# A graph layer in one TensorE queue: the warm-up on zeros becomes 3 wide and 75 narrow products

## What is computed

```
xn = layernorm(x)
q, k, v = (xn @ w.T + b  for w in wq, wk, wv)
q2, k2, v2 = (… @ wi.T + bi for wiq, wik, wiv)            # 16 heads of 64
mask = -inf [384, 384]; mask[src, dst] = softplus(weight of the edge's type)   # 12,288 edges
gnn = softmax(q2 k2.T / 8 + mask) v2 @ wo.T + bo
mix = (sum(phi(xn Wq + bq) * phi(xn Wk + bk)) per head) * (xn Wv + bv) @ Wo + bo
x = x + gnn + mix
x = x + base(layernorm(x)) + conv[e](up[e](relu(down[e](layernorm(x)))))
```

## Time and profile before

| | us |
|---|---|
| median of 3 runs | 499.51 |
| lowest, highest | 494.93, 501.0 |
| the profiled execution, its own time | 493.77 |
| its span, first to last instruction | 491.8 |
| TensorE busy | 468.4 (95%) |
| DVE, ACT, POOL busy | 338.6, 256.0, 160.4 |
| mean granted TensorE clock | 0.976 |

### The profile page before, as it was taken

The page is one execution under the profiler, slowest core; times in us unless marked ns, Lnnn a source line. Parts: engine busy times, 40 slices in busy tenths (PEclk is TensorE's granted clock), DMA queues, the critical chain, the costliest instruction groups (busy, mean ns, idle before and its releaser), DMA issues.

```text
span 491.8 us, 7278 instructions
## 1 busy us (share of the span) xinstructions
PE 468.4 (95%) x2505; PEld 431.0 (88%) x2505; DVE 338.6 (69%) x773; ACT 256.0 (52%) x419; POOL 160.4 (33%) x186
## 2 busy tenths in 40 slices
PE   7999999429999999999999999999999999999996
PEld 5999999219999988899999999999998888888885
DVE  5879975027674535566889797888867885487294
ACT  4444432004332324577897887978876363154170
POOL 5447767756767640100212012120224200040100
PEclk9999999658999999999999999999999999999999
DMA  8878776125673575258677657676669864301463
GB/s 302 259 242 229 233 215 142 41 60 127 168 192 84 186 270 180 81 171 245 220 226 228 217 155 261 186 224 219 206 232 313 320 220 146 112 2 42 132 254 129
DMA packets 39656, 91.85 MB, mean 187 GB/s; under 512 B 7250, under 2 KB 21298, under 8 KB 39492
## 3 DMA queue, kind: packets, MB, share of 16 engines
q1 hardware_dynamic: 34852, 85.38, 55.4%
q0 software_dynamic: 4256, 5.09, 3.3%
q10 hardware_dynamic: 512, 0.92, 0.5%
HBM read 77.90 MB, written 13.47 MB: 186 GB/s over the span
## 4 chain that ended last, share of the span: by engine, by line
PE 83%; DVE 5%; issue 4%; DMA 3%; ACT 3%; SPq 0%; POOL 0%; DVEq 0%; ACTq 0%
PE PS L1314 31%; PE PS L1324 27%; PE PS L1319 15%; PE PS L1444 3%; PE PS L1374 2%; PE PS L1568 1%; PE PS L1432 1%; DMA turn<-U 1%; DMA U<-turn 1%; DVE w_lo L925 1%; PE PS L1302 1%; DVE U L1101 1%; ACT U L700 1%; DVE probT_lo L1066 1%; PE PS L1572 1%
## 5 line engine op out<-in xcount | busy, mean ns | idle before, releaser
L925 DVE TENSOR_TENSOR w_lo<-raw,w_hi 128x1024 fp32r<-128x1024 f32 x85 | 103.8, 1233 | 45.2 <-ACT w_hi L594 38.4
L594 ACT ACTIVATE w_hi<-raw 128x1024 fp32r<-128x1024 f32 x86 | 90.0, 1054 | 74.2 <-PE PS L1324 47.3
L510 POOL DMA_INDIRECT table<-evalue,where x96 | 103.5, 1078 | 51.4 <-issue 31.9
L1314 PE MATMUL PS<-xT_lo,w_hi 128*128 128x384 f32 x320 | 64.4, 339 | 8.9 <-issue 8.9
L1314 PE MATMUL PS<-xT_hi,w_hi 128*128 128x384 f32 x320 | 64.5, 339 | 4.8 <-issue 4.8
L1314 PEld LDWEIGHTS PS<-xT_lo,w_hi 128*128 128x128 f32 x320 | 56.9, 191 | 10.7 <-issue 10.7
L1319 PE MATMUL PS<-xT_hi,w_lo 128*128 128x384 f32 x320 | 63.9, 340 | 1.4 <-issue 1.3
L1314 PEld LDWEIGHTS PS<-xT_hi,w_hi 128*128 128x128 f32 x320 | 56.7, 190 | 6.8 <-issue 6.8
L1319 PEld LDWEIGHTS PS<-xT_hi,w_lo 128*128 128x128 f32 x320 | 57.2, 191 | 2.2 <-issue 2.2
L639 ACT ACTIVATE T_hi<-PS,cst 128x384 fp32r<-128x384 f32 x24 | 13.8, 575 | 61.7 <-remote 26.7
L995 DVE SCALAR_TENSOR_TENSOR T_lo<-PS,cst,T_hi 128x384 fp32r<-128x384 f32 x24 | 14.7, 614 | 37.6 <-issue 20.9
(11 more groups left out here) (241 smaller groups left out, 802.7 us busy)
## 6 DMA issues: line engine op xcount, KB each, us to landing
raw<-weights SPq DMA_DIRECT2D x84, 512.0 KB
turn<-U SPq DMA_DIRECT2D x16, 576.0 KB, 3.7
U<-turn SPq DMA_DIRECT2D x64, 144.0 KB, 3.0
U<-key_dram SPq DMA_DIRECT2D x32, 192.0 KB
mask<-weights SPq DMA_DIRECT2D x9, 512.0 KB
table<-Q SPq DMA_DIRECT2D x4, 576.0 KB, 9.5
V<-conv SPq DMA_DIRECT2D x4, 512.0 KB, 5.2
U<-table POOLq DMA_DIRECT2D x3, 576.0 KB, 6.5
```

The lines of the kernel that those rows point to most:

```text
L510: pool.indirect_dma_start(tables[g], bass.IndirectOffsetOnAxis(ap=where[:, k:k + 1], axis=0), evalue[:, k:k + 1], None, bounds_check=N * N ...
L594: act.activation(w_hi[slot][:], raw[slot][:], ACT.Copy).then_inc(hi_ready[slot], 1)
L925: dve.tensor_tensor(w_lo[slot][:], raw[slot][:], w_hi[slot][:].bitcast(F32), ALU.subtract).then_inc(lo_ready[slot], 1)
L1314: pe.matmul(o, w_hi[slot][:, k * P:(k + 1) * P], src[part][:, k, :], start=(k == 0 and part == 0), stop=False)
```

## The change

The warm-up is 3 products of the old form and then 75 of a new one: 32 columns of weights over all 128 partitions (so 32 rows of result), times 64 columns of zeros, into the first corner of the same bank. They have no waits and no signals. `QUAD` is 32, `HD` is 64, `P` is 128 and `HALF` is 512. TensorE's list has 78 products before the transposes in place of 17, and nothing else in any list is different.

```diff
-WARM = 17
+WARM = 3
+NARROW = 75
...
             pe.wait_ge(warm_ready, 1)
             for n in range(WARM):
                 pe.matmul(PS[:, 0, :], w_lo[2][:, 0:P], w_lo[2][:, P:P + HALF], start=True, stop=True)
+            for n in range(NARROW):
+                pe.matmul(PS[0:QUAD, 0, 0:HD], w_lo[2][:, 0:QUAD], w_lo[2][:, P:P + HD], start=True, stop=True)
 
             pe.wait_ge(ident_ready, 2)
             pe.wait_ge(xn_first, 1)
```

## The result

| | before | after |
|---|---|---|
| median of the first comparison, 6 runs each | 498.74 | 501.27 |
| lowest, highest | 491.29, 501.0 | 496.6, 504.47 |
| the profiled execution, its own time | 493.77 | 502.25 |
| its span | 491.8 | 500.2 |
| mean granted clock | 0.976 | 0.968 |

Ratio 1.0148, 95% interval 1.0103 to 1.0193. It is taken over the faster runs of each kernel alone, and where holes differ from run to run such a choice can favour either side; by the medians of all six runs the ratio is 1.0051. I had forecast 478 us. So the change looks 0.5 to 1.5% slower; the experiments show that this number is not the change's.

The account below looks back on a forecast made before the run. TensorE was taken to lack instructions at a code border near 87 us. Profiled 493.8 - 20 (hole, net) + 0.5 (start) = 474, taken as 478 because the runs' median is 5.7 us higher; range 470 to 505 us.

Parts of the forecast that it names:

- The start: Warm-up before the transposes: 75 narrow pairs at 55 to 60 ns end by 7.0 to 7.4 us, delaying nothing.
- the cover: TensorE's wait until 8.35 us for the first normalised rows hides the zeros, up to 73 ns a pair.
- The late clock: Transposes and first jobs run at 1.2 GHz if narrow products don't raise the clock: 0 to +3.5 us, taken 0.5.
- the 1.7 us for jobs at the lower level: First jobs after a late clock rise: 19.6 us at mean clock 0.91, as seen after the hole, costs 1.7 us.
- the 1.8 us for the transposes: The 12 transposes on the chain at most double in time if the clock stays low: 1.8 us more.
- The hole: TensorE starved of instructions from 87 to 111 us: 20.0 us lost plus 1.7 of clock, 21.7; net gain taken 20.
- The hole therefore begins at a border between two pieces of code: At 87 us TensorE runs out of issued instructions after its code's fourth border; the next piece comes only at 129.9 us.
- 122 instructions more: 61 more pairs before the first job move every code border 10.6 us earlier; hole gone or mostly gone: 0.48.
- a sign of being wrong: Borders standing near 9, 30, 53, 73 and 95 us with the hole elsewhere: moving code only deals the cards again.
- the meeting: Near 83.65 us a code border coincides with something else, such as a slow SP issue or POOL scattering; moved borders undo it.
- Rival 1: The hole stays, same length, at the fourth border or another: 500 us; staying or half of it has chance 0.36.
- Rival 2: A second hole where new borders meet SP and POOL work, 21.7 us each: 521 us; second or longer hole 0.16.

Follow-up runs that it names:

- e10: Kernel before without its scatters, one product of 512 columns as the whole warm-up and no narrow ones: 471.76 us.
- e8: Kernel before without its scatters, warm-up of 17 wide products left as it was: 471.27 us (470.61 to 471.90).
- e1: Kernel before, unedited, profiled a second time: 498.19 us (493.47 to 501.20).
- e15: Changed kernel without scatters, 3 wide and 140 narrow products in place of 75, on another chip: 471.07 us.

## Why the prediction failed

**The start: right.** Zeros that end under the cover (forecast 7.0 to 7.4 us, measured 7.26), 55 to 60 ns a pair (56), the first job near 12.4 (12.30), the clock up before the jobs. Net forecast +0.5 us; measured -0.4 on quiet ground. That the cover ends at 73 ns a pair was not tested, since the pairs turned out at 56 and, with the clock up, at about 33.

**The late clock: mis-sized.** +3.5 us as the upper end; e10 has 0.5 us. The 1.7 us for jobs at the lower level did not arise, since the transposes had raised the clock by then, and the 1.8 us for the transposes were 0.3 to 0.7.

**The hole: right in its size, wrong in its cause.** I priced it at 21.7 us; without the scatters the profiled execution is 23.1 us faster and the median about 26. The step that failed is "The hole therefore begins at a border between two pieces of code". One trace showed one hole at one border, and I took a coincidence for a place. From it I derived that 122 instructions more would move or undo it, and gave 0.48 to that. What the runs showed in its place: the holes need POOL's scatters (471.0 us without them, 497.5 with them), and they begin at other instructions in every execution, also of the same program. The code queue is not shown to matter: its pieces come each 256 instructions with the holes and without them.

The prediction had named this outcome as a sign of being wrong. In the changed kernel the pieces of q8 start at 15.4, 32.1, 52.7, 75.6 and 95.4 us, all but the first within 3 us of the forecast of 9, 30, 53, 73 and 95. The hole is elsewhere, at 111.1. Single waits of "issue" reach 2.1 us, and the last scatter starts at 183.2 us where 165 was the bound.

**What was in view and not used.** TensorE's pace came back at 110.4 us, but no piece of q8 came between 84 and 129.9. If the lack of a piece had stopped TensorE, its arrival should have started it again. (The hole is in the 8th and 9th slice of the earlier trace rows, not in the 9th and 10th as the prediction says; its times are right.) The two slices of the hole stand in the stretch of the scatters, 28 to 175 us, and nowhere else is there one of this size. I named the scatters as one partner of the meeting and then went on with the other. And the runs of before spread over 6 us. Without the scatters six runs agree within 1.3 us (e8), so the spread was the mark of something random, which a change of the program's layout need not touch.

**The rivals.** Rival 1 had the result (no change, about 500 us) with 0.36. Its first reason, something in the fifth piece as such, is wrong. Its second, a rate of such meetings that no layout escapes, is near to what the runs show, and so is its remark that the runs may merely scatter; I gave it the smaller chance. Rival 2, two holes, is what the first profile of the changed kernel showed, though at 502.25 us and not 521, since the second hole was short; e1 has two without the change, so the number of holes is no sign of it.

**What stays open.** Why an issued indirect transfer of POOL makes TensorE's products come at steps of 0.7 us for up to 26 us at a time, and why some executions escape. It is shown that it needs the transfers, that half as many cost less while half the elements in each do not, that the edges need not reach the tables, and that a busy POOL without transfers is harmless. That it needs the indirect form is only made likely, and the number of transfers is not separated from how densely they follow one another. Fewer scatters of more columns would be the way to use this; it was not tried, since two columns in one transfer would need the duplicates between them marked as well.

## What to carry to other kernels

A stall that the profile puts to "issue" and that stands in one trace has no place until a second trace of the same program shows it again; profile the unchanged kernel twice before reasoning on where it stands. When a run's spread is as large as the effect, take the random part out (here the scatters) and measure the change on what is left: 6 runs of each then agree within 1.3 us, where 18 and 70 leave several us open. A transfer's cost can lie on an engine that neither issues it nor waits for it. And a cause that is said to stop an engine must also be seen to end when the engine goes on.

## What the runs showed of the hardware that I had not expected

- 96 indirect transfers from POOL cost TensorE about 26 us of 497 without a semaphore wait between them; 96 pairs of memsets with about as much work on POOL cost nothing (470.8 us).
- An indirect transfer is 32 packets, with 128 elements or with 64, and costs no less with 64 (503.5 against 498.0 us, ratio 1.0137).
- Narrow pairs of 32 by 64 columns take 56 ns at 1.2 GHz, close to 64 columns at that rate (53 ns), so weight load and product overlap at this size too; and in e15 the clock rose under them as under wide ones, at about 5 us. The Trainium skill, "TensorE: Matmul & The Clock Gate", section "Wait — 56ns, not 53.3ns?", has 62 ns a product with the ucode decoder; these pairs are below it, at the upper level with about 33 ns (e15) clearly so, and by that page's two cases the other one holds here.
- 24 transposes after 6 us of idleness took the clock from the lower level to the upper (e10, 421 to 272 ns). The Trainium skill, same page, section "Part 4: PE-mode transpose", says that transposes in TensorE's transpose mode don't engage the full clock. The kernel issues these with `pe.transpose`; if that is this mode, which the trace doesn't name, the run disagrees.
- The same warm-up found the clock up earlier or later: 17 wide products took 5.67 us in one execution and 6.89 in e8. The first job began at 12.43 and 12.74 us.
